# A graph network's second layer: ScalarE fetches one gather tile in every 16 chunks instead of one in every 32

## The reference

```python
        H = jnp.einsum('ni,rio->rno', h, W)
        msg = (H[etype, src] + b[etype]) * norm
        out = jax.ops.segment_sum(msg, dst, num_segments=h.shape[0])
        return jax.nn.relu(out)
...
    h = jnp.maximum(_layernorm(x, axis=-1), 0.0)
    x = x + _L1_gnn_ref(h, src, dst, edge_type_8, edge_weight1, L1_gnn_W, L1_gnn_b)
```

## Time and profile before

| | |
|---|---|
| Time, median of 3 runs | 7919.92 us (7915.28 to 7920.59) |
| Profiled execution, own time | 7916.95 us |
| Its span, first to last instruction | 7915.1 us |
| Busy: PE, PEld | 6812.1 us (86%), 5262.4 us (66%) |
| Busy: POOL | 5850.2 us (74%) |
| Busy: DVE, ACT | 4295.3 us (54%), 2361.7 us (30%) |
| Layer 2, first gather to last scatter | from 4059.84 to about 7882 us |

### The profile page before, as it was taken

How to read it: one execution, slowest core, us unless ns; L and a number is a source line. 1 busy time by engine, 2 the same in 40 slices (tenths; PEclk the granted TensorE clock), 3 DMA queues, 4 the chain that set the end, 5 groups by cost and what they waited for, 6 DMA issues and landing times. The chain is left out here.

```text
span 7915.1 us, 215516 instructions
## 1 busy us (share of the span) xinstructions
PE 6812.1 (86%) x53038; PEld 5262.4 (66%) x53038; DVE 4295.3 (54%) x15013; ACT 2361.7 (30%) x7307; POOL 5850.2 (74%) x6213
## 2 busy tenths in 40 slices
PE   7999999999999999999978887787888887788777
PEld 6666666666666766666666666666666666666666
DVE  5445444454444544544455555555555555555555
ACT  5444444444444444444430000000000000000000
POOL 4777777777777777777757777777777777777776
PEclk8999999999999999999988889888888889988998
DMA  5333333333333333333322222222222222222222
GB/s 145 86 87 87 86 87 86 87 87 86 87 87 86 87 86 86 87 86 87 86 84 56 56 56 56 56 56 56 56 56 56 56 56 56 56 56 56 56 56 77
DMA packets 630304, 585.32 MB, mean 74 GB/s; under 512 B 306227, under 2 KB 505147, under 8 KB 629228
## 3 DMA queue, kind: packets, MB, share of 16 engines
q0 software_dynamic: 197856, 251.86, 15.3%
q1 hardware_dynamic: 422268, 325.27, 14.1%
q10 hardware_dynamic: 9600, 1.60, 0.1%
HBM read 558.88 MB, written 19.27 MB: 73 GB/s over the span
## 5 line engine op out<-in xcount | busy, mean ns | idle before, releaser
L617 POOL DMA_INDIRECT shared<-p_tab,idx x3128 | 2952.4, 944 | 1032.2 <-issue 1029.1
L617 POOL DMA_INDIRECT rows_place<-h_tab,idx x3055 | 2883.3, 944 | 945.3 <-issue 838.5
L1220 PE MATMUL bank<-shared,rows_place 128*128 128x256 f32 x6110 | 1803.2, 446 | 613.9 <-DMA rows_place<-h_tab,idx 602.6
L1220 PEld LDWEIGHTS bank<-shared,rows_place 128*128 128x128 f32 x6110 | 1273.0, 218 | 876.8 <-DMA rows_place<-h_tab,idx 659.4
L1037 DVE SCALAR_TENSOR_TENSOR shared<-bank,key,late 128x256 f32<-128x256 f32 x3128 | 1291.8, 476 | 808.4 <-PE bank L1222 667.4
L779 ACT ACTIVATE h_place<-bank 128x256 f32<-128x256 f32 x782 | 300.4, 384 | 3474.9 <-PE bank L1222 2840.5
L1131 PE MATMUL bank<-h_sb,w_tile 128*128 128x128 f32 x6256 | 908.6, 288 | 69.3 <-DVE h_sb L941 0.9
L1131 PEld LDWEIGHTS bank<-h_sb,w_tile 128*128 128x128 f32 x6256 | 759.3, 191 | 279.4 <-DVE h_sb L941 279.4
L941 DVE TENSOR_SCALAR h_sb<-bank,be_col 128x128 f32<-128x128 f32 x782 | 273.9, 350 | 1236.5 <-PE bank L1124 1236.5
L1150 PE MATMUL bank<-wn_half,h_sb 128*128 128x128 f32 x6256 | 890.8, 285 | 0.0
L1233 PE MATMUL bank<-h_place,w_rel_sb 128*128 128x64 f32 x6256 | 848.0, 293 | 0.0
(11 more groups left out here) (96 smaller groups left out, 6362.8 us busy)
## 6 DMA issues: line engine op xcount, KB each, us to landing
rows_place<-in_dst_c SPq DMA_DIRECT2D x782, 192.0 KB
h_place<-h_tab SPq DMA_DIRECT2D x6272, 0.5 KB
shared<-in_edge_cols SPq DMA_DIRECT2D x782, 128.0 KB
shared<-p_tab,idx POOLq DMA_INDIRECT x3128
h_place<-h_tab ACTq DMA_DIRECT2D x3072, 0.5 KB
rows_place<-h_tab,idx POOLq DMA_INDIRECT x3055
qr_f<-qr_tab SPq DMA_DIRECT2D x782, 36.0 KB
idx<-in_src_t SPq DMA_DIRECT2D x393, 8.0 KB
```

Source lines behind the costliest of these rows:

```text
L617: pool.indirect_dma_start(out=rows_of[s][:, t, :], out_offset=None, in_=table, in_offset=bass.IndirectOffsetOnAxis(ap=idx[k][:, s * TC + t ...
L1220: pe.matmul(bank[s][:, 0:RW], there, hot_rel[s % 2][:, t, :], start=(t == 0), stop=(t == TC - 1))
```

## The change

ACT now takes a tile of every superchunk. It is tile 1 of chunk u = 13, beside SP's tile 0, and POOL gathers only tiles 2 and 3 of that chunk; chunk u = 15 is gathered whole. ACT's row numbers come in SP's list, whose DMA now brings 2 x 128 numbers, and ACT's own list load is gone. With each chunk's copies ACT fetches 8 rows (`feed_step` with lead 2: its last 8 rows follow the copies of u = 11; SP's, with lead 0, stay in its step u = 13). ACT fetches the first 4 pieces of 8 rows before its first copy of the layer (`feed_first`), SP its first 2 as before. At the layer's start SP issues the list load after the wait for `h_stored[3]` alone, and waits for the other three after it. PE waits at u = 13 for the rows of both.

```diff
-        fed_rows = h[2]
-        act_fed_rows = h[3][:, 2, :]
-        act_fed_ids = h[3][0:1, 3, :].bitcast(i32)
+        fed_rows = h[2][:, 0:4, :].rearrange("p (k f) d -> p k f d", f=2)
...
+        def feed(eng, f, lone, piece, landed):
+            _, at = nc.values_load_multi_w_load_instructions(
+                fed_ids[lone.half][0:1, f * P + piece * FED_ROWS:f * P + (piece + 1) * FED_ROWS], engines=(eng.engine,),
...
+            for k, row in enumerate(at):
+                p = piece * FED_ROWS + k
+                eng.dma_start(fed_rows[p:p + 1, lone.half, f, :], h_tab[ds(row, 1), :]).then_inc(landed[lone.half], 16)
+
+        def feed_step(eng, f, lead, u, lone, after, landed):
+            first = FED_AT - lead - SUP + 1
+            if u - first < SUP:
+                feed(eng, f, lone, u - first, landed)
+            elif after:
+                if u == first + SUP:
+                    eng.wait_ge(fed_ids_landed, 16 * after.ids_turn + 16)
+                    hold(eng)
+                feed(eng, f, after, u - first - SUP, landed)
+
+        def feed_first(eng, f, lead, m, landed):
+            eng.wait_ge(fed_ids_landed, 16 * Lone(m, 0, 0).ids_turn + 16)
+            hold(eng)
+            for piece in range(SUP - 1 - FED_AT + lead):
+                feed(eng, f, Lone(m, 0, 0), piece, landed)
...
@@ SP
-                sp.dma_start(fed_ids[lone.half], src_t[:, ds((lone.k * SUP + FED_AT) * TC, 1)].rearrange("p o -> o p"),
+                sp.dma_start(fed_ids[lone.half], src_t[:, ds((lone.k * SUP + FED_AT) * TC, 2)].rearrange("p o -> o p"),
...
+                    feed_step(sp, 0, 0, u, lone, after, sp_row_landed)
+                sp.wait_ge(h_stored[3], 16 * ((NG - 3 + HB - 1) // HB))
                  load_ids(Lone(m, 0, 0))
+                for k in range(3):
+                    sp.wait_ge(h_stored[k], 16 * ((NG - k + HB - 1) // HB))
+                feed_first(sp, 0, 0, m, sp_row_landed)
@@ POOL
-                gather(c, k, two, h_tab, rows, scattered, idx1_landed, rows_landed, range(u == FED_AT or act_fed(u, lone), TC))
+                gather(c, k, two, h_tab, rows, scattered, idx1_landed, rows_landed, range(2 if u == FED_AT else 0, TC))
@@ ACT
-                elif (at - 1) * ACT_ROWS < P:
-                    feed(at - 1)
+                feed_step(act, 1, 2, u, lone, after, act_row_landed)
...
             with act.Fori(0, passes) as m:
+                feed_first(act, 1, 2, m, act_row_landed)
                 superchunks(act, m, copy_sums)
@@ PE
                 if u == FED_AT:
-                    pe.wait_ge(fed_row_landed[lone.half], 16 * P * lone.turn + 16 * P)
-                if act_fed(u, lone):
-                    pe.wait_ge(act_row_landed, 16 * P * lone.act_turn + 16 * P)
+                    pe.wait_ge(sp_row_landed[lone.half], 16 * P * lone.turn + 16 * P)
+                    pe.wait_ge(act_row_landed[lone.half], 16 * P * lone.turn + 16 * P)
```

More of the change, by code:

```diff
@@ L55, in gnn_two_layers @@
     FED_AT = 13
-    ACT_ROWS = 5
-    ACT_FED_AT = SUP - 1
     NQ = (NCH + SL - 1) // SL
@@ L177, in gnn_two_layers @@
         tile_sums = sb("tile_sums", [P, D])
-        fed_rows = h[2]
-        act_fed_rows = h[3][:, 2, :]
-        act_fed_ids = h[3][0:1, 3, :].bitcast(i32)
-        fed_ids = [h[3].rearrange("p j d -> p (j d)")[0:1, k * P:(k + 1) * P].bitcast(i32) for k in range(2)]
+        fed_rows = h[2][:, 0:4, :].rearrange("p (k f) d -> p k f d", f=2)
+        fed_ids = [h[3].rearrange("p j d -> p (j d)")[0:1, 2 * k * P:2 * (k + 1) * P].bitcast(i32) for k in range(2)]
         bank = [ctx.enter_context(nc.psum_tensor(f"bank{k}", [P, 512], f32)) for k in range(8)]
@@ L236, in gnn_two_layers @@
         pass1_ready, pass1_step = sem("pass1_ready"), sem("pass1_step")
-        fed_ids_landed, fed_row_landed = sem("fed_ids_landed"), slot_sems("fed_row_landed", 2)
-        act_ids_landed, act_row_landed = sem("act_ids_landed"), sem("act_row_landed")
+        fed_ids_landed = sem("fed_ids_landed")
+        sp_row_landed, act_row_landed = slot_sems("sp_row_landed", 2), slot_sems("act_row_landed", 2)
         block = ctx.enter_context(nc.Block())
@@ L344, in __init__ @@
             def __init__(self, m, two, half):
-                self.m, self.half, self.two = m, half, two
+                self.m, self.half = m, half
                 self.k = two * 2 + half
-                self.act_turn = m * (NSUP // 2) + two
                 self.turn = m * LONE_USES[half] + two
@@ L362, in superchunks @@
                 step(Chunk(m, quad, u % SL), u, quad % 2, m * (NQ // 2) + quad // 2, Lone(m, NSUP // 2, 0), None)
-        def act_fed(u, lone):
-            return u == ACT_FED_AT and lone.half == 1
         def tiles_gathered(c, u, lone):
-            if c.slot == ACT_FED_AT % SL:
-                return (c.m * (TC * SLOT_USES[c.slot] - NSUP // 2) + lone.two * (2 * TC * SUP // SL - 1)
-                        + (TC * ((lone.half * SUP + u) // SL + 1) - act_fed(u, lone)))
             if c.slot != FED_AT % SL:
                 return TC * c.turn + TC
-            return (c.m * (TC * SLOT_USES[c.slot] - (NSUP + 1)) + lone.k * (TC * SUP // SL - 1)
-                    + (TC * (u // SL + 1) - (u >= FED_AT)))
+            return (c.m * (TC * SLOT_USES[c.slot] - 2 * (NSUP + 1)) + lone.k * (TC * SUP // SL - 2)
+                    + (TC * (u // SL + 1) - 2 * (u >= FED_AT)))
+        def feed(eng, f, lone, piece, landed):
+            _, at = nc.values_load_multi_w_load_instructions(
+                fed_ids[lone.half][0:1, f * P + piece * FED_ROWS:f * P + (piece + 1) * FED_ROWS], engines=(eng.engine,),
+                min_val=0, max_val=NPAD - 1, skip_runtime_bounds_check_because="a source node's number is below the number of nodes")
+            for k, row in enumerate(at):
[15 more added lines that the diff above has]
+                feed(eng, f, Lone(m, 0, 0), piece, landed)
         def quads_after_first(eng, m, step):
@@ L532, in _ @@
             passes = number_of_passes(sp)
-            for k in range(HB):
-                sp.wait_ge(h_stored[k], 16 * ((NG - k + HB - 1) // HB))
             def load_ids(lone):
-                sp.dma_start(fed_ids[lone.half], src_t[:, ds((lone.k * SUP + FED_AT) * TC, 1)].rearrange("p o -> o p"),
+                sp.dma_start(fed_ids[lone.half], src_t[:, ds((lone.k * SUP + FED_AT) * TC, 2)].rearrange("p o -> o p"),
                              allow_slow_non_contiguous=True).then_inc(fed_ids_landed, 16)
[L541 to L548, removed]
             def layer1_pass(m):
-                FIRST = FED_AT - SUP + 1
                 def step(c, u, k, two, lone, after):
@@ L762, in _ @@
                     normalise_mid(g - 1)
[L765 to L772, removed]
             def copy_sums(c, u, k, two, lone, after):
@@ L780, in copy_sums @@
                 act.activation(w_sums[half][:, k, :], bank[c.slot][0:R, RW:RW + W], ACT.Copy).then_inc(sums_copied[c.slot], 1)
[L781 to L786, removed]
-                elif (at - 1) * ACT_ROWS < P:
-                    if at == 1:
-                        act.wait_ge(act_ids_landed, 16 * lone.act_turn + 16)
-                        hold(act)
-                    feed(at - 1)
+                feed_step(act, 1, 2, u, lone, after, act_row_landed)
             for k in range(HB):
@@ L1209, in scatter @@
                 if u == FED_AT:
-                    pe.wait_ge(fed_row_landed[lone.half], 16 * P * lone.turn + 16 * P)
-                if act_fed(u, lone):
-                    pe.wait_ge(act_row_landed, 16 * P * lone.act_turn + 16 * P)
+                    pe.wait_ge(sp_row_landed[lone.half], 16 * P * lone.turn + 16 * P)
+                    pe.wait_ge(act_row_landed[lone.half], 16 * P * lone.turn + 16 * P)
                 pe.wait_ge(sums_copied[s], c.turn + 1)
                 for t in range(TC):
[L1215 to L1219, removed]
+                    there = fed_rows[:, lone.half, t, :] if u == FED_AT and t < 2 else rows[s][:, t, :]
                     pe.matmul(bank[s][:, 0:RW], there, hot_rel[s % 2][:, t, :], start=(t == 0), stop=(t == TC - 1))
```

## The result

The kernel after takes 7884.94 us (median of 6 runs, 7883.86 to 7887.79) against 7916.53 us before (6 runs, 7914.85 to 7920.59): ratio 0.9959, 95% interval 0.9947 to 0.9971. That is 31.6 us less; the spans of the two profiled executions differ by 7915.1 - 7884.5 = 30.6.

The account below looks back on a forecast made before the run. POOL was taken to bound layer 2, its gathers 1.2487 us from start to start. 25 fewer save 31.2 us, all else costing nothing: 7919.92 - 31.2 = 7888.7 us, range 7882 to 7912.

Parts of the forecast that it names:

- The bound and the price: Layer 2: POOL, paced by its own instructions, makes 25 fewer gathers at 1.2487 us each, saving 31.2 us.
- ACT's step: ACT's copy, register load and 8 row DMAs for each chunk: 4.2 us, below POOL's 4.839, with the load taken as 0.78.
- the long load: ACT's register load if long, as some of its loads of 5 numbers: 0.58 us more, a step of 4.8.
- ACT as the bound from 4.84 on: Rival: ACT's copies and rows in one stream decide from 4.84 us; at 4.9 the time is 7937; chance 0.07.
- The start: Layer's start: ACT fetches 4 pieces first, its first copy some 5 us late, made up at 0.64 a chunk; costs nothing.
- Chunk 13: PE's wait still ends on SP; POOL keeps 3.4 us of lead. Rival of partial loss there: 7904, chance 0.13.
- PE's waits for h_place: PE's waits for the fetched rows, 126.6 us in 42 before, get longer by some 1.2 us each.
- SP: SP's waits for POOL's tiles, 11.7 us in 32 chunks before, shrink to 8 to 10 left.
- The shared generator: Rule: sequencers issuing such DMAs share one locked descriptor generator, so SP would wait behind ACT's DMAs; rows show at most 0.005 each.
- SP's rival: SP becomes the bound from 0.03 to 0.04 us more per DMA; at 0.06 the time is 8039; chance 0.06.

Follow-up runs that it names:

- f6: The kernel after with SP's row numbers stored one number off, ACT's in place, in executions about 1.5 times as long: 12345 us, 1.0617 of before.

## Why the prediction was right

It said 7888.7 for the median and measured was 7884.9; the change was to save 31.2 us and saved 31.6. Of the 3.8 us between the two times 3.4 come from the kernel before, whose median is 7916.5 over 6 runs and was 7919.9 over the first 3. That the savings agree to 0.4 us is in part luck: in the two traces the gathers end 28.9 us earlier and 1.7 us come from behind them, and the medians of the kernel before differ by 3 us from one set of runs to the next. Point by point:

- **The bound and the price.** Right, and shown from both sides: 49 gathers more cost 65.6 us, 48 fewer save 58.5, 25 fewer saved 31.6. That is 1.34, 1.22 and 1.26 us a gather against the 1.2487 read from the spacing; an error of 3 us in a time is 0.06 of it for the first two and 0.12 for the third.
- **ACT's step.** 4.2 us were predicted, 4.19 measured. The load was taken as 0.78 and is 0.723; the choice between the short and the long one, which I made by SP's rows, was right. Its stated upper end, 0.58 more for the long load, was far too low: 8 numbers out of place take 1.95 us, not 1.3. The error here is that I bounded the load of 8 by the long load of 5. Had the numbers stood out of place, the time would have been 8463 and far outside the range.
- **ACT as the bound from 4.84 on.** Right as a rival, and its price too: 48 us was given for a step of 4.9, and 128 us came at a step of 5.0 (782 x 0.16 = 125), 578 at one of 5.57.
- **The start.** ACT's first copy was to be 5 us late and to catch up at 0.64 a chunk. It came at 4077.67, and PE's first scatter ends at 4071.73 + 0.60: 5.3 late, made up in ten copies. It costs nothing, as said.
- **Chunk 13.** That PE's wait still ends on SP is right (3.97 us against 3.93). That 3.4 us of lead are left, and that ACT may lag 6.6, was read from one superchunk. 2.5 us at PE's start were enough to cost 27 us in all. From there to the end of chunk 14's scatter PE took 11.5 us in the place that was read, where the granted clock was 0.56, and 12.8 us in the kernel after where it was 0.51 (6767.84 to 6780.61). With ACT's rows one step later it took 8.6 where the clock was 0.79 (5936.36 to 5944.91). So the margin moves with the clock, and the prediction has no term for that. The mechanism was right, the margin was mis-sized by reading it in one place. The forecast held because ACT's rows come before SP's, so little of the margin was used beyond the 1.25 us of the missing gather; one stop of 0.8 us in the kernel after shows that little was to spare.
- **PE's waits for h_place.** Predicted 1.2 us longer each, measured 137.1 / 42 = 3.3 against 126.6 / 42 = 3.0; over all 49 it is 3.1 against 2.9. This was an error in reasoning: the wait runs from the end of PE's own chunk 12 to SP's rows, and POOL's missing gather enters neither. The 1.25 us shows up as lost lead of POOL, not as waiting of PE.
- **SP.** Its waits are 222.0 us of 3500 against 262.3:

```profile
SPq L430 <- DMA rows_place<-h_tab,idx: 222.0, 113, 2.9
```

  In 32 chunks 9.8 are left, where 8 to 10 were predicted. 32 row DMAs take 15.87 as before.
- **The shared generator.** The rule of the Trainium skill ("Perfetto Trace Analysis", the HWDGE instruction) was given as SP's rival. With 32 row DMAs of ACT in four chunks, SP's DMAs take 228 ns in the middle and 303 at most, 228 and 326 before. Without any DMA of ACT in the layer they take 228 and 288, and SP's waits are 228.0 us of 3500 in place of 222.0: ACT's DMAs cost SP at most 6 us of 3500, 0.3 in 32 chunks. That the whole program's time stays the same with or without them (0.5 us) says little on this, as SP isn't the bound. If the two wait for each other, it is hardly to be seen here.

## What to carry to other kernels

Where one engine issues without a gap, the price of what it issues is the distance from start to start (1.25 us here, not the 0.94 of its busy time), and work taken off it is paid back in full as long as the engines that take it over stay below its pace and deliver in time. So read the pace of each of them in the units of the bound, with everything that stands in its stream: 0.7 us more in ACT's step of 4.19 would have turned the gain into a loss of 97 us. Read a step and a margin over many turns of the loop, its end included, and not in one place: ACT's 5.4 us were 5.57, and the 3.4 us of lead were gone where the granted clock was 0.50.

Before moving a list of numbers that an engine loads into registers, look where each load begins: a piece of 8 that begins at a multiple of 8, or 4 past one, took 0.72 us here, and one that begins a single number later 1.95.

## What the hardware showed that was not expected

- A register load of 8 numbers (4 bytes each) takes 0.72 us on ACT where it begins at a multiple of 8 numbers and 1.95 us where it begins one number later; of 5 numbers 0.72 at a multiple of 4 and 1.29 elsewhere. A load of 8 that begins 4 numbers past a multiple of 8 takes 0.72 too (f6). A spare load of a single number takes 0.57 and made a step 0.7 us longer; ACT's loads of 8 took 0.55 beside it, which nothing here explains.
- PE's 8 matmuls of a chunk take 1.99 us at the full granted clock and 3.78 at 0.50. Where the clock is low right behind a wait of PE, the engine that runs ahead of PE loses its lead: with ACT's rows one step later 34 of 35 us of POOL's stops lie in such places.
